# A graph network layer on one core: four of a chunk's 25 banks are counted and copied during the products of the chunk in front

## What is computed

```python
msg = x[src] + edge_attr
agg = jax.ops.segment_sum(msg, dst, num_segments=N)
h = jax.nn.relu(agg @ W1 + b1) @ W2 + b2
...
h = jax.nn.gelu(h)
return h + x
...
x = _layernorm(x + _L0_gnn_ref(...), axis=-1)
```

## Time and profile before

| | |
|---|---|
| three runs | 790.06 us median (789.42 to 791.05) |
| the profiled execution | 790.67 us, of which its span 788.9 |
| granted TensorE clock, mean | 0.961 |
| PE matmul busy | 689.8 us, 87% |
| DVE busy | 661.5 us, 84% |
| ACT busy | 393.2 us, 50% |
| POOL busy | 101.7 us, 13% |

### The profile page before, as it was taken

How to read it: one execution, slowest core, us unless ns; L and a number is a source line. 1 busy time by engine, 2 the same in 40 slices (tenths; PEclk the granted TensorE clock), 3 DMA queues, 4 the chain that set the end, 5 groups by cost and what they waited for, 6 DMA issues and landing times.

```text
span 788.9 us, 25577 instructions
## 1 busy us (share of the span) xinstructions
PE 689.8 (87%) x9447; PEld 620.9 (79%) x9447; DVE 661.5 (84%) x1161; ACT 393.2 (50%) x858; POOL 101.7 (13%) x69
## 2 busy tenths in 40 slices
PE   0976899999999999999999999999999999999750
PEld 0964888988889888888888888898888988788630
DVE  5786989989899898999989898898988989725585
ACT  0934266435663356533565346643466434624464
POOL 2042201111011110111101110011101111000000
PEclk9985899999999999999999999999999999999965
DMA  6968356256562564635646356464563545331005
GB/s 152 303 205 257 100 191 195 76 174 199 181 188 94 169 202 163 192 110 169 199 149 196 123 169 199 132 201 128 177 199 117 200 131 188 108 127 39 0 0 162
DMA packets 88985, 123.61 MB, mean 157 GB/s; under 512 B 8572, under 2 KB 84446, under 8 KB 88763
## 3 DMA queue, kind: packets, MB, share of 16 engines
q1 hardware_dynamic: 82220, 116.30, 45.9%
q0 software_dynamic: 5744, 5.38, 2.6%
q10 hardware_dynamic: 1000, 1.65, 0.8%
HBM read 119.23 MB, written 4.03 MB: 156 GB/s over the span
## 4 chain that ended last, share of the span: by engine, by line
PE 63%; ACT 17%; issue 9%; DMA 4%; DVE 4%; ACTq 2%; DVEq 1%; POOLq 0%
PE bank L736 37%; ACT counts L551 12%; PE bank L711 12%; PE bank L662 7%; PE bank L793 3%; PE bank L783 3%; ACT below L507 2%; DMA begins<-listed,tile_slot 2%; DMA agg<-in_src_dram 1%; PE bank L676 1%; ACT sums L527 1%; DVE x_lo L960 1%; DMA near<-listed,row_slot 1%; DVE pool_m L1253 1%; ACT pool_m L618 1%
## 5 line engine op out<-in xcount | busy, mean ns | idle before, releaser
L551 ACT CAST counts<-bank 128x490 fp32r<-128x490 f32 x625 | 311.0, 697 | 304.7 <-PE bank L711 304.7
L736 PE MATMUL bank<-counts,x_hi 128*128 128x250 f32 x1225 | 290.9, 282 | 31.3 <-ACT counts L551 31.3
L736 PE MATMUL bank<-counts,x_lo 128*128 128x250 f32 x1225 | 287.3, 279 | 0.0
L1017 DVE TENSOR_TENSOR pool_m<-value_row,turned_lo 128x3328 bf16<-128x3328 bf16 x125 | 236.1, 1889 | 35.1 <-ACT turned_key L533 20.9
L736 PEld LDWEIGHTS bank<-counts,x_hi 128*128 128x128 f32 x1225 | 231.5, 189 | 35.1 <-ACT counts L551 35.1
L736 PEld LDWEIGHTS bank<-counts,x_lo 128*128 128x128 f32 x1225 | 232.2, 190 | 0.0
L711 PE MATMUL bank<-pool_m 128*128 128x98 bf16 x3125 | 203.3, 211 | 5.9 <-DVE pool_m L1017 4.1
L711 PEld LDWEIGHTS bank<-pool_m 128*128 128x128 bf16 x3125 | 162.6, 99 | 46.8 <-ACT counts L551 27.5
L1017 DVE TENSOR_TENSOR pool_m<-value_row,turned_key 128x2548 bf16<-128x2548 bf16 x125 | 184.9, 1479 | 0.0
L662 PE MATMUL bank<-edges,onehot 128*32 128x128 f32 x3228 | 122.1, 286 | 7.2 <-DVE onehot L930 3.4
L456 POOL DMA_INDIRECT near<-listed,row_slot x27 | 54.9, 2033 | 526.5 <-DVE row_slot L981 483.1
(11 more groups left out here) (152 smaller groups left out, 402.1 us busy)
## 6 DMA issues: line engine op xcount, KB each, us to landing
edges<-in_edge_attr_dram SPq DMA_DIRECT2D x134, 768.0 KB, 5.5
out_dram<-pool_m SPq DMA_DIRECT2D x6, 512.0 KB
agg<-in_dst_dram SPq DMA_DIRECT2D x1, 768.0 KB
agg<-in_src_dram ACTq DMA_DIRECT2D x1, 768.0 KB
listed<-agg ACTq DMA_DIRECT2D x1, 768.0 KB
begins<-listed,tile_slot POOLq DMA_INDIRECT x28, 4.1
near<-listed,row_slot POOLq DMA_INDIRECT x27
w<-in_L_gnn_W_dram SPq DMA_DIRECT2D x2, 128.0 KB, 2.6
```

The lines of the kernel that those rows point to most:

```text
L551: nc.scalar.copy(counts[:, :, k * nodes:(k + 1) * nodes], cps[k % RING][:, 0:nodes * NT].rearrange("p (n q) -> p q n", q=NT)).then_inc(ban ...
L736: last = nc.tensor.matmul(sps[:, 0:CHUNK], part[:, q, :], counts[:, q, :], start=(q == 0 and part is x_hi), stop=(q == NT - 1 and part is ...
L1017: last = dve.tensor_tensor(to[b % MARKED], values[:, :, 0:n, :].to_broadcast([P, BLOCKS_B, n, INTER]), of.to_broadcast([P, BLOCKS_B, n, IN ...
```

## The change

For every chunk but chunk 0 the counting of banks 0 to 3 moves ahead, into the products of the chunk before: one bank each ahead of tiles 26, 31, 36 and 41. Their copies stand on ScalarE behind the keys, ahead of the wait for `chunk_summed`. So that they don't overwrite what the products read, `counts` has 290 columns. An even chunk uses columns 0 to 249. An odd chunk's banks 0 to 3 go to columns 250 to 289, the others where they were, and its products read columns 40 to 289; the sums then stand rotated in `sps`, so `add_chunk` needs two instructions, of 40 and of 210 columns. In the counting phase 21 banks are left, and the table of the halves has them four banks apart in place of five. The first four banks of chunk 0 are counted and copied ahead of the loop.

Room for the 40 columns comes from two moves. The weights W1 and W2 are loaded into the marks' third buffer, behind a wait for bank 15 of the last chunk. And the matrix of ones lies in a part of `begins`, written by GpSimd behind its last gather.

```diff
+AHEAD = 4
+AHEAD_AT = (26, 31, 36, 41)
-HALVES_AT = (1, 6, 11, 16, 21)
-SUMS_AT = ({8: 0, 18: 1}, {3: 2, 13: 3})
-TURNS_AT = ({13: 0, 23: 1}, {8: 2, 18: 3})
+HALVES_AT = (5, 9, 13, 17, 21)
+SUMS_AT = ({10: 0, 18: 1}, {6: 2, 14: 3})
+TURNS_AT = ({15: 0, 23: 1}, {11: 2, 19: 3})
...
+    NODES = BANK * PAIR
+    AHEAD_N = AHEAD * NODES
...
-        counts = sb("counts", [P, NT, CHUNK], F32R)
+        counts = sb("counts", [P, NT, CHUNK + AHEAD_N], F32R)
...
+            sp.wait_ge(banks_done, (CHUNKS - 1) * BANKS + (MARKED * BPB + CREDIT))
             sp.dma_start(w1[:, :], W1).then_inc(weights_loaded, 16)
...
+            pool.wait_ge(begins_loaded, (CHUNKS + 3) * 16)
+            pool.memset(ones, 1.0).then_inc(ones_ready, 1)
...
+            def copy_bank(c, k, odd):
+
+                act.wait_ge(banks_done, c * BANKS + (k + 1 + CREDIT))
+                at = k * NODES + (CHUNK if odd and k < AHEAD else 0)
+                nc.scalar.copy(counts[:, :, at:at + NODES],
+                               cps[k % RING][:, 0:NODES * NT].rearrange("p (n q) -> p q n", q=NT)
+                               ).then_inc(banks_free, 1)
+
+            def copy_chunk(c, odd, first, at):
...
                 act.wait_ge(chunk_summed, c + 1)
...
+                for k in range(AHEAD, BANKS):
+                    copy_bank(c, k, odd)
...
                     copy_keys(p * 2 + (odd + 1))
                     if odd:
                         copy_sums(p * PER_PAIR + (LEAD + PER_PAIR - 1), 0)
+                    for k in range(AHEAD):
+                        copy_bank(p * 2 + (odd + 1), k, 1 - odd)
...
+            def count_bank(c, k):
+
+                b = k // BPB
+                if k % BPB == 0:
+                    pe.wait_ge(marks_ready, c * BATCHES + (b + 1))
+                if k >= RING:
+                    pe.wait_ge(banks_free, c * BANKS + (k + 1 - RING))
+                for i in range(BANK):
...
+                last.then_inc(banks_done, 1)
...
+                for k in range(AHEAD, BANKS):
+                    count_bank(c, k)
...
+                    if q in AHEAD_AT and more:
+                        count_bank(c + 1, AHEAD_AT.index(q))
+                    at = AHEAD_N if odd else 0
                     for part in (x_hi, x_lo):
-                        last = nc.tensor.matmul(sps[:, 0:CHUNK], part[:, q, :], counts[:, q, :],
+                        last = nc.tensor.matmul(sps[:, 0:CHUNK], part[:, q, :], counts[:, q, at:at + CHUNK],
...
+                if odd:
+                    at = agg[:, bass.ds(c * CHUNK, AHEAD_N)]
+                    dve.tensor_tensor(at, at, sps[:, CHUNK - AHEAD_N:CHUNK], ALU.add)
+                    at = agg[:, bass.ds(c * CHUNK + AHEAD_N, CHUNK - AHEAD_N)]
+                    dve.tensor_tensor(at, at, sps[:, 0:CHUNK - AHEAD_N], ALU.add).then_inc(chunk_added, 1)
```

More of the change, by code:

```diff
@@ L197, in gnn_kernel @@
         iota_i = begins[:, 0:P]
+        ones = begins[:, P:2 * P].bitcast(F32)
         junk = sb("junk", [P, SPAN])
@@ L436, in _ @@
             pool.iota(pair_i[:, :], [[PAIR * PAIRS, CHUNKS + 3]], base=0, channel_multiplier=PAIR)
-            pool.memset(ones_b[:, :], 1.0)
-            pool.memset(ones[:, :], 1.0).then_inc(consts_ready, 1)
+            pool.memset(ones_b[:, :], 1.0).then_inc(consts_ready, 1)
             for a, b in PIECES:
@@ L562, in _ @@
                         copy_sums(p * PER_PAIR + (LEAD + PER_PAIR - 1), 0)
-            copy_chunk(CHUNKS - 1, FULL - 1 - GPC, SUMS_AT[0])
+                    for k in range(AHEAD):
+                        copy_bank(p * 2 + (odd + 1), k, 1 - odd)
+            copy_chunk(CHUNKS - 1, 0, FULL - 1 - GPC, SUMS_AT[0])
             copy_sums(FULL - 1, 0)
@@ L698, in _, with count_chunk @@
             turn_sums(LEAD - 1, (LEAD - 1) % GPC)
-            def count_chunk(c, p, odd, halves, keys=True):
-                first = p * PER_PAIR + LEAD
[L703 to L716, removed]
+            def count_bank(c, k):
[5 more added lines that the diff above has]
+                for i in range(BANK):
+                    n = (k % BPB) * BANK + i
+                    last = nc.tensor.matmul(cps[k % RING][:, i * KEYS:(i + 1) * KEYS],
+                                            mark_lo[b % MARKED][:, n // INTER, :, n % INTER],
+                                            mark_key[b % MARKED][:, n // INTER, :, n % INTER],
+                                            start=(i == 0), stop=(i == BANK - 1),
+                                            skip_group_check=True)
+                last.then_inc(banks_done, 1)
+            def count_chunk(c, p, odd, halves, more=True):
+                first = p * PER_PAIR + LEAD
+                for k in range(AHEAD, BANKS):
+                    count_bank(c, k)
                     if k in HALVES_AT[:halves]:
@@ L725, in count_chunk @@
                         turn_sums(first + j, j % GPC)
-                    if k == KEYS_AT and keys:
+                    if k == KEYS_AT and more:
                         pe.wait_ge(keys_ready, c * 2 + 2)
@@ L740, in _ @@
             pe.wait_ge(x_split, NT // PIECE)
+            for k in range(AHEAD):
+                count_bank(0, k)
             with pe.Fori(0, PAIRED) as p:
@@ L743, in _ @@
                     count_chunk(p * 2 + odd, p, odd, PER_PAIR)
-            count_chunk(CHUNKS - 1, PAIRED, 0, HPC, keys=False)
+            count_chunk(CHUNKS - 1, PAIRED, 0, HPC, more=False)
+            pe.wait_ge(ones_ready, 1)
             pe.wait_ge(cover_in, 1)
             pe.wait_ge(keys_ready, 2 * CHUNKS)
-            nc.tensor.matmul(turn_ps[:, 0:TURNS + 2], ones[:, :], st[:, COVER:COVER + TURNS + 2], start=True, stop=True
+            nc.tensor.matmul(turn_ps[:, 0:TURNS + 2], ones, st[:, COVER:COVER + TURNS + 2], start=True, stop=True
                              ).then_inc(cover_summed, 1)
@@ L810, in _ @@
                 pe.wait_ge(mean_in, k + 1)
-                nc.tensor.matmul(turn_ps[:, k:k + 1], ones[:, :], st[:, k:k + 1],
+                nc.tensor.matmul(turn_ps[:, k:k + 1], ones, st[:, k:k + 1],
                                  start=True, stop=True, skip_group_check=True).then_inc((mean_summed, root_in)[k], 1)
@@ L1019, in mark_batch, with add_chunk @@
                 last.then_inc(marks_ready, 1)
-            def add_chunk(c, groups):
+            def add_chunk(c, groups, odd):
                 dve.wait_ge(chunk_summed, c + 2)
                 dve.wait_ge(edges_added, groups + 2)
-                at = agg[:, bass.ds(c * CHUNK, CHUNK)]
-                dve.tensor_tensor(at, at, sps[:, 0:CHUNK], ALU.add).then_inc(chunk_added, 1)
+                if odd:
[3 more added lines that the diff above has]
+                    dve.tensor_tensor(at, at, sps[:, 0:CHUNK - AHEAD_N], ALU.add).then_inc(chunk_added, 1)
+                else:
+                    at = agg[:, bass.ds(c * CHUNK, CHUNK)]
+                    dve.tensor_tensor(at, at, sps[:, 0:CHUNK], ALU.add).then_inc(chunk_added, 1)
             for g in range(GPC):
@@ L1082, in even @@
                     mark_batch(c + 1, 2)
-                    add_chunk(c, first + 2)
+                    add_chunk(c, first + 2, 0)
             def odd(c, p):
@@ L1106, in odd @@
                 mark_batch(c + 1, 2)
-                add_chunk(c, first + 5)
+                add_chunk(c, first + 5, 1)
             with dve.Fori(0, PAIRED) as p:
@@ L1154, in _ @@
             flag = dve.value_load(flag_i[0:1, 0:1], min_val=0, max_val=1)
-            add_chunk(CHUNKS - 1, FULL - 1)
+            add_chunk(CHUNKS - 1, FULL - 1, 0)
             dve.wait_ge(chunk_added, CHUNKS + 1)
```

18 lines of the change are left out of this document (7 added, 11 removed).

## The result

The changed kernel takes 791.87 us (median of 10 runs, 790.80 to 793.16), the kernel before beside it 789.70: a ratio of 1.0024, 95% interval 1.0016 to 1.0031. It is 0.24% slower, where I had forecast 1.4% slower and a range that began at 788. The time lies in that range and the sign is right, but the size is not: +11.3 us was foretold, +2.2 measured.

What follows compares the result with a forecast made beforehand. TensorE was taken as the fullest engine, with ScalarE ending the counting phases. Products +32.9 us and counting -21.6 us summed to +11.3, giving 801.4 us on the median of 790.06; range 788 to 812.

Steps and rivals of the forecast that it cites:

- What bounds the kernel: Over a pair of 49.60 us TensorE is busy 47.12, with some 2.5 to give back; ScalarE sets the counting phase's end.
- a bank at 0.282: TensorE's price for counting one bank, in us, read from one stretch of the counting phase.
- ScalarE's excess is 0.34 us a chunk: In counting, ScalarE's 13.23 us against TensorE's own 12.89; this excess is what the change can remove outright.
- The odd chunk: Counting, from first counted bank (T) to first product (P), takes 12.13 us, 1.10 less; marks come in time.
- The even chunk: Counting, first bank (T) to first product (P): 12.60 us, 0.63 less; TensorE waits 0.76 at bank 20 for marks.
- The products: Four banks at 0.282 plus 0.06 per return to a product: 1.37 us a chunk, 24 chunks, +32.9 us.
- The last chunk: Its counting has four halves and no keys; bank 20 waits for marks at about 8.5, some 1.5 us less.
- Edits at nothing: Moved weight loads and the ones written on GpSimd cost nothing; uncovered, each would cost one load or memset, once.
- 1, VectorE in time: VectorE has marks ready in even chunks too, 0.75 us less in each of 11: 793.1 us; chance 0.14.
- rival 2: The 0.20 behind a half is a wait for ScalarE's copy, which the change removes; half costs 0.60: 786.2; chance 0.14.
- 3, the whole weight load exposed at a switch: Returning from a bank to products costs 0.19 us, not 0.06: 12.5 us more, 813.9; chance 0.14.
- 4: ScalarE's order puts the keys' copies ahead of the four banks' copies, which could slip past the products; given nothing.

Runs made afterwards that it cites:

- run 1: Changed kernel with an unused 96-byte gap ahead of pool_m, so that it starts at a multiple of 256 bytes: 788.74 us, ratio 0.9991 to the kernel before.
- run 3: Kernel before with only the changed kernel's three tables (halves, sums, turns), no bank counted ahead: 780.93 us, ratio 0.9888.
- run 4: Changed kernel with two banks ahead (tiles 36 and 41) instead of four, pool_m aligned to 256 bytes: 780.93 us, ratio 0.9881 to the kernel before.
- run 7: Changed kernel with two banks ahead, pool_m aligned, and even chunks' product-sum addition behind marks batches 3 and 4 on VectorE: 774.40 us, ratio 0.9803 to the kernel before.
- run 5: Changed kernel, not aligned, with VectorE's places, one-hots and marks batches 3 and 4 ahead of the product-sum addition in even chunks: 783.58 us, ratio 0.9918 to the kernel before.
- run 8: Changed kernel, pool_m aligned, its four banks ahead in one row at tile 36 instead of four separate tiles: 783.82 us, ratio 0.9931 to the kernel before.
- run 2: Kernel before with an unused 160-byte gap ahead of pool_m, so that it starts 160 bytes past a multiple of 256: 792.21 us, ratio 1.0029.

## Why the prediction was wrong

The step that failed is the sum of what the change removes from the counting phases. I had it at 21.6 us; the phases gave 11 x 0.76 + 12 x 1.68 + 1.9 = 30.4. The price of the banks in the products was too high by 3.1 us besides, and the address of `pool_m` had no term at all.

**What bounds the kernel: right only for four banks, and wrong in one price.** I said that TensorE has little to give back and that work moved within it gains nothing. For the four banks of the change that holds: they cost 7.8 us beside the tables alone (runs 1 and 3). As a rule it does not: two banks ahead cost nothing (run 4), and gained 6.5 us once the wait for marks was gone (run 7). What moves also leaves ScalarE's 25 copies in the counting phase, and as long as these end the phase, that is a gain. And the first price in the list, a bank at 0.282 from (326.14 - 324.73) / 5, was too high. In that stretch bank 6 had to wait for copy 2, which began at 325.18 and lasted 0.58, to 325.76. Bank 6 began at 325.81, 0.36 behind bank 5, where the steps from bank 2 to bank 5 are 0.23 to 0.25. I had taken a stretch with a little waiting in it for TensorE's own pace. In the new phases, where copies are not in the way, a bank takes 0.26 in the mean, in a row among products 0.23. So "ScalarE's excess is 0.34 us a chunk" was too small by about 25 x 0.022 = 0.55, and there was more to gain from the phase than I allowed.

**The odd chunk: -1.10 forecast, -1.68 measured; the largest miss, 12 x 0.58 = 7.0 us.** Two terms of its sum were mis-sized. Bank 22 came at T + 9.50 in place of 9.87 (the price of a bank). And from the last copy's start to P passed 361.17 - 360.51 = 0.66, not 0.88. The 0.88 was that of the even chunk; in the odd one it had been 361.36 - 360.56 = 0.80. Here are an odd chunk's last copy before and after, two timelines of ScalarE:

```profile
360.56 0.75 ACT L551 CAST counts<-bank 128x490 fp32r<-128x490 f32 x1
```

```profile
360.51 0.61 ACT L558 CAST counts<-bank 128x490 fp32r<-128x490 f32 x1
```

The copy's own duration shrank, over all copies from 697 to 611 ns. The single copies of the traces show the pattern. Behind every pause of ScalarE a copy lasts 0.58 us, and in a row without a pause each lasts 0.01 or so longer than the one before, up to 0.86: the starts are 0.463 apart, the ends 0.475. The counting phases of before are nearly one such row. The new ones have pauses, since TensorE now holds ScalarE up behind the halves, and so the last copy is a short one. P follows the end of the last copy by 0.05 to 0.06 us in both. What in the engine makes the durations grow was not tried.

**The even chunk: -0.63 forecast, -0.76 measured.** The mechanism, the wait that moves to VectorE's list, was right with its place, and bank 20 came 0.10 later than worked out. The wait was longer than foretold (1.08 against 0.76), because TensorE arrived sooner. The phase was shorter all the same, since from bank 20 to P passed 336.85 - 333.46 = 3.39, not 12.60 - 8.98 = 3.62: again the price of a bank and the shorter last copy. Run 5 shows the wait's cause.

**The products: +1.37 a chunk forecast, +1.24 measured, 24 x 0.13 = 3.1 us.** 0.34 for a bank should have been 0.31; run 8 splits it into 0.23 and 0.08 where I had 0.28 and 0.06.

**The last chunk** gave 1.9 in place of 1.5 (0.4 us), and the even ones together 11 x 0.13 = 1.4. These four misses are 11.9 us: on the terms of my own sum the changed kernel should have come out at -0.6 us.

**What no term had: the move of pool_m, +2 to 3 us.** "Edits at nothing" looked at the wait and at the memset, and not at what the new width of `counts` does to all that lies behind it. The Trainium skill, "DMA: Bandwidth & Descriptors", section "How a descriptor splits into AXI transactions", says that a descriptor which does not start at a multiple of 256 bytes begins with a transaction from the boundary below it, and that the unused bytes of this transaction take beats of 32 bytes like the others. By that rule an estimate for a row of 512 bytes starting at 160 is 21 beats in place of 16, 0.76 of the rate. Runs 1 and 2 agree in direction, with 290 / 347 = 0.84.

So the sign came out right by luck. Four misses of size, all in one direction, took away the 11.3 us, and what made the kernel slower is a term that I did not have: without the shift the change is within 0.2% of the kernel before (run 1). The rest of "Edits at nothing" holds: with the gap the kernel's last stretch is as long as before (104.28 and 104.17 us).

**The rivals.** 1, VectorE in time, fell: TensorE waits for batch 4 in every even chunk, the last too (0.45 there). 2, the gap of 0.20 behind a half as a wait for ScalarE, fell: 325.75 - 324.95 = 0.80 stands also behind the first half of the new phase, where the bank needs no copy of this phase. That rival 2 had the odd chunk at 1.68 less, as measured, is coincidence: it got there by a half of 0.60 and a wait for marks, and in the odd chunks neither is there. 3, the whole weight load exposed at a switch, fell: a return costs 0.08, not 0.19. 4 fell: the copies of the four banks start 0.44 us after their banks, within the products. None of the rivals was that the two halves of the change, its tables and its banks ahead, pull in opposite directions. I priced the counting phase as one, and so could not see that its tables alone are worth 8.9 us; only run 3 told them apart.

## What to carry to other kernels

Take the price of an instruction from a stretch in which its engine waits for nobody, and check it on a second stretch: an error of 0.02 us in a step that occurs 600 times is 12 us, as much as this change was forecast to move. If a change alters both a schedule and the amount of work in a phase, price and run each alone, and try less of the move as well as all of it: here two banks ahead did better than four (runs 1, 4, 5 and 7). When an array grows, look at where the arrays behind it start that transfers touch. And before moving work to another phase of the same full engine, look for idle waits in that engine into which a piece of its own list fits.

## What the runs showed of the hardware

- Output rows of 512 bytes leave SBUF at 347 GB/s from a start at a multiple of 256 bytes and at 290 from one 160 past it, in two kernels alike (runs 1 and 2).
- Five matmuls of 98 columns with their weights take 0.26 us in the mean between halves of edges and 0.23 in a row among products; a return from them to a float32r product costs 0.08 (run 8).
- ScalarE's copies of 128 x 490 keep a step of 0.46 to 0.47 us, but a single one lasts 0.57 to 0.86 us from start to end: 0.58 behind a pause, and longer the longer the row without one. The reader starts 0.05 to 0.06 us behind that end.
- When a matmul waits for two semaphores, the releaser that the profile names may be the one long met: the wait for marks stood as "ACT counts" in ten of the changed kernel's twelve even chunks behind the first, and as "DVE pool_m" with two banks ahead (run 4).
- One gather by GpSimd took 7.96 us in place of 1.35 in the six kernels in which it began 0.07 us behind the start of a batch of marks on VectorE, and not 0.18 ahead of it; the cause was not tried (run 5).
